# Cross-attention and a routed expert layer in one program: twelve expert blocks moved in among the last attention slots

## The reference

```python
# x, ctx: (64, 128, 256); 16 heads of 16; 8 experts, 2 per token, hidden 512
x = x + xattn(layernorm(x), ctx, W_q, b_q, W_k, b_k, W_v, b_v, W_out, b_out)
x = x + ffn(layernorm(x), W1, b1, W2, b2, Wr, br)

# xattn, per sequence and head
q, k, v = heads(x_q @ W_q.T + b_q), heads(x_kv @ W_k.T + b_k), heads(x_kv @ W_v.T + b_v)
out = softmax(q @ k.T / 4) @ v            # then @ W_out.T + b_out

# ffn, per token
logits = x @ Wr + br                      # the 2 largest of 8, softmax over the two
a, g   = split(x @ W1[e] + b1[e])
y_e    = (silu(a) * g) @ W2[e] + b2[e]
out    = gate_1 * y_e1 + gate_2 * y_e2
```

## Time and profile before

| | us |
|---|---|
| median of 3 runs | 1299.19 (1297.65 to 1301.61) |
| the profiled execution | 1298.25 |
| its span, first to last instruction | 1296.40 |
| TensorE busy | 1178.3 (91%) |
| VectorE busy | 999.1 (77%) |
| ScalarE busy | 807.0 (62%) |
| GpSimd busy | 620.9 (48%) |

### The profile page before, as it was taken

How to read it: one execution, slowest core, us unless ns; L and a number is a source line. 1 busy time by engine, 2 the same in 40 slices (tenths; PEclk the granted TensorE clock), 3 DMA queues, 4 the chain that set the end, 5 groups by cost and what they waited for, 6 DMA issues and landing times. The chain is left out here.

```text
span 1296.4 us, 38380 instructions
## 1 busy us (share of the span) xinstructions
PE 1178.3 (91%) x12538; PEld 1042.2 (80%) x12539; DVE 999.1 (77%) x2926; ACT 807.0 (62%) x1640; POOL 620.9 (48%) x728
## 2 busy tenths in 40 slices
PE   5899999999999999740499999999999999999986
PEld 4677777777777777530499999999999999999986
DVE  5788888888888887734478888888888888887763
ACT  5676666666666666412376766766667666676552
POOL 5346666666666665542034344344443444432333
PEclk9999999999999999855699999999999999999998
DMA  5122333233333222216767777777777677776553
GB/s 173 41 82 89 98 96 96 98 98 103 103 102 103 94 71 70 70 60 204 252 162 180 192 163 181 178 170 191 165 180 183 165 191 167 180 184 156 149 151 37
DMA packets 106527, 175.81 MB, mean 136 GB/s; under 512 B 13040, under 2 KB 81840, under 8 KB 106288
## 3 DMA queue, kind: packets, MB, share of 16 engines
q1 hardware_dynamic: 77376, 135.47, 32.3%
q0 software_dynamic: 26592, 36.46, 17.1%
q10 hardware_dynamic: 2448, 2.44, 0.6%
HBM read 126.21 MB, written 47.60 MB: 134 GB/s over the span
## 5 line engine op out<-in xcount | busy, mean ns | idle before, releaser
L1306 POOL DMA_INDIRECT out_rows<-y_gated,block_tokens x142 | 263.7, 1857 | 433.5 <-DVE y_gated L1278 333.2
L1064 PE MATMUL bank<-block_T_hi,w_hi 128*128 128x256 f32 x1136 | 328.2, 289 | 10.6 <-DVE block_T_lo L1252 10.6
L1066 PE MATMUL bank<-block_T_hi,w_lo 128*128 128x256 f32 x1136 | 321.3, 283 | 0.0
L1065 PE MATMUL bank<-block_T_lo,w_hi 128*128 128x256 f32 x1136 | 321.2, 283 | 0.0
L1064 PEld LDWEIGHTS bank<-block_T_hi,w_hi 128*128 128x128 f32 x1136 | 215.7, 190 | 12.6 <-DVE block_T_lo L1252 7.9
L1065 PEld LDWEIGHTS bank<-block_T_lo,w_hi 128*128 128x128 f32 x1136 | 216.0, 190 | 0.0
L1066 PEld LDWEIGHTS bank<-block_T_hi,w_lo 128*128 128x128 f32 x1136 | 215.7, 190 | 0.0
L491 ACT ACTIVATE probs_T<-bank 128x512 f32<-128x512 f32 x256 | 132.2, 603 | 98.3 <-PE bank L322 98.3
L1160 ACT ACTIVATE act_hi<-act 128x512 fp32r<-128x512 f32 x142 | 89.8, 632 | 150.7 <-DVE act L1262 150.7
L1262 DVE SCALAR_TENSOR_TENSOR act<-bank,block_b,silu_a 128x256 f32<-128x256 f32 x284 | 124.3, 480 | 75.1 <-ACT silu_a L1141 45.5
L599 DVE TENSOR_REDUCE row_max<-bank 128x4 f32<-128x512 f32 x256 | 158.9, 683 | 22.4 <-PE bank L303 22.4
(11 more groups left out here) (151 smaller groups left out, 2504.2 us busy)
## 6 DMA issues: line engine op xcount, KB each, us to landing
w_raw<-in_L_ffn_W SPq DMA_DIRECT2D x71, 1024.0 KB
block_rows<-routed_rows SPq DMA_DIRECT2D x71, 272.0 KB, 3.3
x_in<-in_x SPq DMA_DIRECT2D x64, 128.0 KB, 2.4
ctx_T<-in_ctx SPq DMA_DIRECT2D x16, 512.0 KB, 3.9
x_res<-in_x SPq DMA_DIRECT2D x64, 128.0 KB, 2.7
out_rows<-x SPq DMA_DIRECT2D x64, 128.0 KB, 2.3
w_raw<-in_L_ffn_W SPq DMA_DIRECT2D x8, 512.0 KB, 7.8
out_rows<-y_gated,block_tokens POOLq DMA_INDIRECT x142, 4.4
```

The lines of the kernel that those rows point to most:

```text
L1064: mm(dst, w1h[:, k, c, at:at + P], xh[:, k, c, :], start=(c == 0), stop=False)
L1065: mm(dst, w1h[:, k, c, at:at + P], xl[:, k, c, :], start=False, stop=False)
L1066: last = mm(dst, w1l[:, k, c, at:at + P], xh[:, k, c, :], start=False, stop=(c == KC - 1))
L1306: nc.gpsimd.indirect_dma_start(out=out[:, :], out_offset=bass.IndirectOffsetOnAxis(ap=tk[:, u % U, t:t + 1], axis=0), in_=yg[:, u % 2, t, ...
```

## The change

The two programs become one list per engine. The expert blocks are split in two sets. Twelve full blocks (M = 12) are taken from the counts of the first 48 tiles (EARLY), whose rows have been scattered by slot 58; a first table for them is computed on VectorE in slots 54 to 57 (`early_blocks`, `early_shares`, `early_owners`, `early_starts`). By the inputs they are 7 blocks of expert 0, 3 of expert 1 and 2 of expert 2. A second table (`late_tables`) gives the other 59 blocks.

Slots 65 to 69 of attention alternate with expert slots 0 to 4 (`k` in the code below). What each engine does for the experts before that stands in `prepare(t)`: SP loads b1 and b2 at slot 56, stores the spare idle rows at 60, loads W1 of block 0 and the rows of blocks 0 and 1 at 62, W1 of block 1 at 64; ScalarE issues the loads of W2, two experts in each of slots 56 to 59, and converts two experts in each of slots 60 to 63, then W1 of block 0. `w2_raw` is gone: W2 is loaded to the place of `w2_lo` and overwritten there by VectorE's subtraction. That place, and those of `w2_hi`, `block_T_hi`, `block_T_lo` and `y_gated`, lie over attention's inputs (`overlaid`); W1's second buffer and the activations lie over q, k, v and the probabilities. Block transposes go to bank 5 instead of bank 4. ScalarE stores the idle rows of the eight experts, two behind each of expert slots 5 to 8, and SP waits for them, for the second table and for all scatters before it loads block 12.

```diff
+M = 12
...
+    def turns(eng, slot, begun):
+
+        for b in range(begun, M):
+            slot(b // U, b % U)
+        with eng.Fori(M // U, NTURN - 1) as i:
+            for u in range(U):
+                slot(i, u)
+        for u in range(NT - U * (NTURN - 1)):
+            slot(NTURN - 1, u)
...
+            def expert_slot(i, u):
+                if has(i, u + 2):
+                    if isinstance(i, int) and blk(i, u + 2) == M:
+                        sp.wait_ge(s_tab, 2)
+                        sp.wait_ge(s_sc, 16 * TOPK * NB)
+                        sp.wait_ge(s_pd, 16 * E)
+                    load_rows(i, u + 2)
+                    load_w1(i, u + 2)
...
+                if t == 62:
+                    sp.wait_ge(s_tab, 1)
+                    sp.wait_ge(s_free, EARLY)
+                    load_w1(0, 0)
+                    load_rows(0, 0)
+                    load_rows(0, 1)
+                if t == NB:
+                    sp.wait_ge(s_pv, count(NB - 1, NCH))
+                    load_w1(0, 1)
...
+            def expert_slot(i, u, between=None):
+                up_half(i, u, 0)
+                if has(i, u + 1):
+                    rows_T(i, u + 1)
+                if between is not None:
+                    ranks_and_logits(between)
+                up_half(i, u, 1)
...
+            for k in range(GB + 1):
+                squares_and_out(NB + 1 + k)
+                expert_slot(k // U, k % U, NB + 1 + k)
+            turns(pe, expert_slot, GB + 1)
...
+                if 56 <= t < 60:
...
+                    for e in range(2 * (t - 56), 2 * (t - 55)):
+                        act.dma_start(w2l[:, e * FC * D:(e + 1) * FC * D].bitcast(F32).rearrange("p (c n) -> p c n", c=FC),
+                                      w2[e].rearrange("(c p) n -> p c n", p=P)).then_inc(s_w2[e], 16)
+                if 60 <= t < 64:
+                    if t == 60:
+                        act.wait_ge(s_vm, NB)
+                    for e in range(2 * (t - 60), 2 * (t - 59)):
+                        act.wait_ge(s_w2[e], 16)
+                        nc.scalar.activation(w2h[:, e * FC * D:(e + 1) * FC * D],
+                                             w2l[:, e * FC * D:(e + 1) * FC * D].bitcast(F32), ACT.Copy).then_inc(s_w2h, 1)
+                if t == NB - 1:
+                    w1_hi(0, 0)
+                if t == NB:
+                    x_hi(0, 0)
...
+            for k in range(GB + 1):
+                last_sums(NB + 1 + k)
+                expert_slot(k // U, k % U, NB + 1 + k)
+            late_tables()
+            turns(dve, expert_slot, GB + 1)
...
+            before()
+            for t in range(NB + 1):
+                slot(t)
+            slot(NB + 1)
+            slot(NB + 2)
+            for i in range(2):
+                pool.wait_ge(s_x2d[i], 16 * (NB // 2))
+            pool.wait_ge(s_dum, 32)
+            for k in range(GB - 1):
+                expert_slot(k // U, k % U)
+                slot(NB + 3 + k)
+            turns(pool, expert_slot, GB - 1)
```

900 lines of the change are left out of this document (500 added, 400 removed).

## The result

| | us |
|---|---|
| kernel before, median of 4 (beside it) | 1300.4 |
| changed kernel, median of 4 | 1267.26 |
| ratio (medians without the execution of 3771 us) | 0.9737 (0.9706 to 0.9769) |
| its profiled execution | 1268.36 |
| its span | 1266.5 |

The forecast was 1320; rival 1 (1262) came about. One execution took 3771 us and is left out of the ratio; nothing of it was seen again, and its cause is not known. The second half of this text shows that in other calls the same kernel takes 1314 us and is slower than before. In what follows "late pattern" is what the prediction calls so; the expectations also say "slow pattern".

What follows compares the result with a forecast made beforehand. TensorE's pace was taken to bound the expert blocks, with 72.4 us unfilled before block 0. Gain 49.5 less 13.5 in the first blocks, then slow blocks: 1298.25 - 36.0 + 55.6 + 2.0 = 1319.9, said as 1320; range 1261 to 1333.

Steps and rivals of the forecast that it cites:

- rival 1: Expert blocks after block 5: GpSimd's late adds catch up, so no lasting slow stretch; time 1262 us, chance 0.24.
- late pattern: Expert blocks from block 7 to 61: VectorE waits for late-landing adds, 10.0 instead of 8.97 us a block, 55.6 us.
- the forecast's mechanism: Expert blocks: late adds' landing releases the next adds and W1 load together, which slows landing again; 10.0 us a block.

Runs made afterwards that it cites:

- before_hold10_gate: Kernel before plus about 10 us of GpSimd powers ahead of block 3's adds, W1 load waiting for a semaphore behind block b - 5's second add: 1342.77 us, ratio 1.052.
- A: Kind of call in which the kernel before took 1299 to 1300 us (median), an attention slot 8.3 us; the changed kernel took 1267.26 us there.
- B: Kind of call in which the kernel before took 1277 to 1279 us (median), an attention slot 7.8 us; the changed kernel took 1314.26 us there.
- after_gate2: Changed kernel with each W1 load waiting until the second add of block b - 5 is fully issued: 1259.97 us, ratio 0.969.
- before_hold10_gate2: Kernel before plus about 10 us of GpSimd powers ahead of block 3's adds, W1 load waiting until block b - 5's second add is fully issued: 1288.66 us, ratio 0.992.
- before_hold10_small_w1: Kernel before plus about 10 us of GpSimd powers ahead of block 3's adds, W1 loads from block 6 cut to 128 of 1024 columns: 1287.48 us, ratio 0.991.

## What to carry to other kernels

A chain that is shorter than its slot by a fifth (here 7.1 us of adds in 8.97) can still have a second stable way of running, if being late puts it beside a large transfer that its own completion releases. Look for such loops, and order the transfer behind the issue that it could overtake; that cost one wait here and was worth up to 77 us. A time from one call says which way the program ran there, not that it always will.

## What the hardware showed

- An indirect add of GpSimd takes 1.54 us to be issued (2.40 beside `w_lo`). A semaphore raised behind it in program order went up at its start (before_hold10_gate: the load left 0.3 us behind that start); one raised by a small instruction that GpSimd itself executes came 0.1 us after the end. With a 1 MB load issued 0.3 us after the second add's start GpSimd waited 6.0 us and more for the landing, with one issued 1.9 us after it 3.7 us. The Trainium skill says that a DMA engine takes turns between its queues packet by packet (DMA: Bandwidth & Descriptors, "Queues, rings and completion order"); that a load beside the adds costs them more than one behind them agrees with it, how much was not to be had from it.
- Beside ten scatters of 128 rows in a row TensorE was held up for 8 us on A and never on B. What it lacked is open. The Trainium skill calls the fetching of the next block of instructions mostly hidden (Runtime: NRT & Kernel Launch, "Instruction fetch mechanics"), and no run here shows the contrary: instruction packets of 16 KB come 11 to 23 us apart in this part of the run, and none between 635.4 and 660.7, but TensorE works again at its pace from 655.9, before the next one, and takes 310 matmuls and weight loads from one to the next, as many as on B between 625.2 and 647.1 (303). So the missing packets look like a result of the delay and not its cause. Why A and B differ in this, and in the pace of attention (8.3 and 7.8 us a slot), stays open.
- In all twenty traces one second add, late in the run, stands 2.5 to 3.5 us behind the first instead of 0.3: at block 56 in the six kernels made from the kernel before, and in those made from the changed one at block 59, or at 63 in the five with the scatters spread. So it goes with the program and not with the kind of call or the rows. In the kernel before it leaves the W1 load only 0.55 us behind the second add (1162.15) in place of some 2.8, and from that block on to the last W1 load the landing takes over 6 us; VectorE feels it six blocks later (four to eight in the others). Where the load waits or is small (after_gate2, before_hold10_gate2, before_hold10_small_w1) the same late add is followed by nothing. So it very likely starts the stretch at the end, by the forecast's mechanism; no kernel without it was run. What it is stays open.
